# Reworked first and last stages, an earlier bias row, and the first MoE weight loaded ahead of the fifth and later x tiles, in a macaron transformer layer

## The reference

```python
x = x + 0.5 * ffn(layernorm(x))            # first MoE stage
x = x + attn(layernorm(x))                 # attention block with its own MLP
x = x + 0.5 * ffn(layernorm(x))            # second MoE stage, same weights

def ffn(x):                                # sq_relu(h) = relu(h)**2
    shared = sq_relu(x @ Ws1) @ Ws2        # 1024 -> 512 -> 1024
    top_vals, top_idx = top_k(x @ Wr, 2)   # 8 experts
    prob = trunc(softmax(top_vals))        # 1 only if a weight reaches 1.0
    return shared + (expert outputs weighted by prob)

def attn(t):
    q, k, v = t @ Wq + bq, t @ Wk + bk, t @ Wv + bv            # 16 heads of 64
    S = (q k^T - dist_scale * |i - j|) / sqrt(64), with a mask on (key, head) pairs
    h = layernorm(t + softmax(S) v @ Wo + bo, ln1)
    return layernorm(relu(h @ W1 + b1) @ W2 + b2 + h, ln2)     # 1024 -> 4096 -> 1024
```

## Time and profile before

| | us |
|---|---|
| median of 3 runs | 1446.87 |
| lowest and highest run | 1446.06, 1447.27 |
| the profiled execution | 1446.01 |
| its span, slowest core (core 6) | 1442.9 |
| its fastest core (core 7) | 1429.0 |
| PE, DVE, ACT busy on core 6 | 1279.6, 787.6, 833.9 |

### The profile page before, as it was taken

One profiled execution on the slowest core, in us unless ns is written; L12 is line 12 of the kernel. 1 busy time (PEld: TensorE's weight loads), 2 busy tenths in 40 slices (PEclk: granted clock), 3 DMA queues, 4 the chain that ended last, 5 costly groups with the idle time before them and its releaser, 6 DMA issues.

```text
span 1442.9 us, 20405 instructions; the slowest of 8 cores (1429.0 to 1442.9 us)
## 1 busy us (share of the span) xinstructions
PE 1279.6 (89%) x6458; PEld 616.9 (43%) x6580; DVE 787.6 (55%) x1272; ACT 833.9 (58%) x1173; POOL 38.3 (3%) x68
## 2 busy tenths in 40 slices
PE   3769879999989999999799999988999999789984
PEld 2334324444433644444346444444544444455442
DVE  5845314554457734459685443786834439680074
ACT  4555447777755766766557567665665666522311
POOL 1010200000000000000000000000000000000000
PEclk9979999999999999999999999999999999999997
DMA  9956999999923521314554222156431323685443
GB/s 229 210 109 133 167 127 128 133 118 128 137 61 106 157 96 64 120 62 147 182 154 146 67 87 92 55 179 201 135 121 62 110 77 85 191 248 176 149 140 109
DMA packets 115216, 187.66 MB, mean 130 GB/s; under 512 B 55822, under 2 KB 92692, under 8 KB 104088
## 3 DMA queue, kind: packets, MB, share of 16 engines
q1 hardware_dynamic: 86536, 154.74, 35.6%
q0 software_dynamic: 28560, 31.45, 17.9%
HBM read 178.86 MB, written 45.09 MB: 155 GB/s over the span
## 4 chain that ended last, share of the span: by engine, by line
PE 70%; DVE 9%; ACT 7%; issue 7%; DMA 3%; SPq 1%; another core or an unknown queue 1%; DVEq 0%; ACTq 0%
PE PS L243 70%; ACT EB L806 2%; DVE AT L846 1%; DMA HT<-SG 1%; DVE EB L812 1%; DVE sm L224 1%; DVE sm L226 1%; DMA VV<-x 1%; ACT RT L842 1%; ACT RT L840 1%; DMA Y<-SG 1%; ACT RT L843 1%; ACT H L1028 1%; SPq L66 1%
## 5 line engine op out<-in xcount | busy, mean ns | idle before, releaser
L806 ACT ACTIVATE EB<-PS 128x1024 bf16<-128x1024 f32 x512 | 520.6, 1021 | 312.7 <-PE PS L243 308.0
L812 DVE TENSOR_TENSOR EB<-EB,DP 128x1024 bf16<-128x1024 bf16 x512 | 352.0, 690 | 414.7 <-ACT EB L806 412.5
L243 PE MATMUL PS<-RG,H 128*128 128x512 bf16 x1251 | 306.7, 381 | 28.3 <-ACT H L1028 8.1
L243 PE MATMUL PS<-EB,VV 128*128 128x512 bf16 x988 | 298.5, 381 | 19.0 <-DVE AT L846 9.1
L243 PE MATMUL PS<-HT,RG 128*128 128x256 bf16 (+1 forms) x1647 | 283.3, 316 | 29.4 <-ACT H L1028 12.2
L243 PE MATMUL PS<-QP,KT 128*128 128x512 bf16 x1007 | 302.3, 380 | 5.4 <-ACT EB L806 3.0
L243 PEld LDWEIGHTS PS<-HT,RG 128*128 128x128 bf16 x1664 | 163.1, 99 | 137.8 <-issue 36.0
L243 PEld LDWEIGHTS PS<-RG,H 128*128 128x128 bf16 x1280 | 124.1, 98 | 186.3 <-issue 43.0
L243 PEld LDWEIGHTS PS<-QP,KT 128*128 128x128 bf16 x1024 | 99.9, 98 | 128.2 <-issue 10.0
L243 PEld LDWEIGHTS PS<-EB,VV 128*128 128x128 bf16 x1024 | 96.9, 98 | 126.7 <-issue 34.1
L1028 ACT ACTIVATE H<-PS,sm 128x256 bf16<-128x256 f32 (+1 forms) x176 | 98.3, 567 | 69.0 <-PE PS L243 68.7
(11 more groups left out here) (124 smaller groups left out, 825.7 us busy)
## 6 DMA issues: line engine op xcount, KB each, us to landing
RG<-wcW SPq DMA_DIRECT2D x64, 1024.0 KB, 5.4
RG<-wcWo SPq DMA_DIRECT2D x8, 1024.0 KB, 8.4
wcW<-W1a POOLq DMA_DIRECT2D x8, 1024.0 KB, 21.6
wcW<-W2a POOLq DMA_DIRECT2D x8, 1024.0 KB, 19.0
Y<-x1sp SPq DMA_DIRECT2D x16, 512.0 KB, 4.2
XT<-x1sp SPq DMA_DIRECT2D x16, 512.0 KB, 4.2
RG<-wcS SPq DMA_DIRECT2D x8, 1024.0 KB, 5.7
out<-Y SPq DMA_DIRECT2D x16, 512.0 KB, 3.3
```

The costliest lines, as they stand in the source:

```text
L243: return s.on("tensor", lambda e: e.matmul(out, lhsT, rhs, start=first, stop=last, skip_group_check=True), wait=wait, inc=inc)
L806: te = s.on("scalar", lambda e: e.activation(eb, po, AF.Exp, bias=-12.0, scale=1.0), wait=[tm, self.e_free[k], self.tok_consts])
L812: self.tok_p[k] = s.on("vector", lambda e: e.tensor_tensor(eb3, eb3, dp, ALU.mult), wait=[te, self.tok_dp])
```

## The change

1. Ws1 is loaded by two POOL DMAs of half its rows; x tiles 4 to 15 on SP wait for the first of them. Ws2 waits for x tile 7 (was 3), Wv for x tile 9 (was 7).
2. `wide` is loaded by eight SP DMAs of 496 columns behind the x tiles, no longer by POOL. `table` runs at k == 16 and also adds the two bias rows (`trw`), with the row's store and the load of GC behind it on SP; these stood after the loop.
3. The POOL load of the first half of Wq waits for the last transpose of stage A (tr2[15]), and the second half of Wk stands behind it.
4. In stage B the first K and Q projections are emitted first; a POOL no-op waits for the first K projection (all four parts) before Wq1 and the casts of `wc`.
5. `out_row` is emitted in `proj_stream` before head pair 6, not after pair 7, and the rest of the Q projections is reordered around it.
6. Squares of the last MoE are ACT instructions (AF.Square) in all blocks. For b = 3 the x1 rows are loaded into four places of KT, with the bias added ahead; `ln3_out` follows its own statistics at once; the MoE runs on tiles (0,1), (2), (3); of the router, the flag is computed from 16 columns, the four table operations follow the flag, and the last tile's two additions stand within the router.

The core of the diff:

```diff
@@ router
+        if mid is not None:
+            mid()
         v(lambda e: e.tensor_single_scalar(self.rden, self.rd, 1.0, ALU.add), [te])
...
-        v(lambda e: e.tensor_tensor(PR3, LT3, bc(self.v2), ALU.is_ge))
-        v(lambda e: e.tensor_tensor(PR3, PR3, bc(self.rw), ALU.mult))
-        v(lambda e: e.tensor_tensor(eq3, eq3, bc(self.rp1), ALU.mult))
-        v(lambda e: e.tensor_add(self.PR, self.PR, self.eq1))
+        v(lambda e: e.tensor_add(self.rden, self.rp1, self.rw))
...
+        t = v(lambda e: e.tensor_reduce(fm, self.rden, AX.X, ALU.max))
@@ phase_a
+                x_tok.append(s.dma("sync", "x%d" % i, xs[i], self.x0_d[128 * i:128 * i + 128, :], wait=wait))
...
+        tws = [s.dma("gpsimd", "ws1%d" % h, as8(sws1)[:, 4 * h:4 * h + 4, :], src1[:, 4 * h:4 * h + 4, :])
+               for h in range(2)]
...
-        load(4, 16)
+        load(4, 16, wait=[tws[0]])
...
-        twd = s.dma("gpsimd", "wide", wide, self.widea_d)
+        twds = []
+        for j in range(0, WIDE, 496):
+            twds.append(s.dma("sync", "wide%d" % (j // 496), wide[:, j:j + 496], self.widea_d[:, j:j + 496]))
...
-            if k == 14:
+            if k == 16:
                 table()
             if k - ROW2 - 1 == 11:
-                for j, w in ((2, self.Wk_d), (3, self.Wq_d)):
...
+                self.tok_ring[2] = s.dma("gpsimd", "r2", as8(self.slot(2)), piece(self.Wk_d, 0, 0),
+                                         wait=x_left[8] + x_left[9])
             if k - ROW2 - 1 == 15:
+                self.tok_ring[3] = s.dma("gpsimd", "r3", as8(self.slot(3)), piece(self.Wq_d, 0, 0),
+                                         wait=x_left[10] + x_left[11] + [tr2[15]])
@@ proj_stream
         for p in range(1, 8):
+            if p == 6:
+                yield from self.out_row(s)
@@ post_rows
+            XT = [self.KT[:, 2 * D * k:2 * D * k + 2 * D].bitcast(F32) for k in range(4)]
+            for tt in range(4):
+                t = self.x1_again(s, b, tt, XT[tt], [self.q_used[31]])
+                txs[tt] = s.on("vector", lambda e, x=XT[tt]: e.tensor_add(x, x, gc[:, D:2 * D]),
+                               wait=[t, self.tok_gc])
...
+            if not self.lagging:
+                self.ln3_out(s, b, HTt, *late)
+                late = None
@@ post_fill
-        for lo in (0, 2):
+        for lo, hi in ((0, 2), (2, 4)) if b < 3 else ((0, 2), (2, 3), (3, 4)):
...
-                th = s.on("vector", lambda e, hf=hf: e.tensor_mul(hf, hf, hf), wait=[t])
+                th = s.on("scalar", lambda e, hf=hf: e.activation(hf, hf, AF.Square), wait=[t])
...
+                tflag, table = self.router(
+                    s, [tlt], 1, lambda: [self.moe_out(s, b, tt, dh, *outs[dh]) for dh in range(2)])
...
+                table()
@@ phase_b
+        for tq in range(4):
+            for _ in self.proj(s, "k", 0, tq):
+                pass
+        for _ in self.proj(s, "q", 0, 0):
+            pass
+
+        s.on("gpsimd", lambda e: e.nop(), wait=[self.tok_k[0]], inc=False)
         self.ring_load(s, self.tok_v_pe)
```

More of the change, by code:

```diff
@@ L244, in mm, with router @@
                                                  skip_group_check=True), wait=wait, inc=inc)
-    def router(self, s, wait, k):
+    def router(self, s, wait, k, mid=None):
         LT3 = self.LT.rearrange("p (t e) -> p t e", e=8)
@@ L772, in proj_stream @@
             yield from self.proj(s, "q", p, 0)
-            if p < 7:
+            if p < 6:
                 for tq in range(1, 4):
                     yield from self.proj(s, "q", p - 1, tq)
-        yield from self.out_row(s)
+        for tq in range(1, 4):
+            yield from self.proj(s, "q", 5, tq)
         for tq, p in ((2, 6), (3, 6), (2, 7), (3, 7)):
@@ L1101, in post_fill @@
                 self.ht_free = [tm, tx]
-                if b == 3:
-                    tflag = self.router(s, [tlt], 1)
-            for tt in (lo, lo + 1):
-                i = 4 * b + tt
+            for tt in range(lo, hi):
+                outs = []
                 for dh in range(2):
```

114 lines of the change are left out of this document (63 added, 51 removed).

## The result

The changed kernel took 1425.99 us (median; 1425.78, 1425.99 and 1427.46), the kernel before, on the same chip, 1446.46. The ratio is 0.9862, with a 95% interval of 0.9842 to 0.9881: 20 us gained, 6 fewer than forecast.

A forecast was written before the change was run, and what follows sets the result against it. PE bounds attention; only stalls at four places could move. The slowest core, 3: 1439.7 - 10.3 - 2 - 2.2 - 1 - 10 = 1414.2, plus 2 for scatter, 3.1 outside and 0.9 to the median: 1420 us; range 1409 to 1434.

The forecast's parts named there:

- The table: Distance table in stage A: ACT's wait for the constant goes; -13 us in core 6, -6.6 core 1, -10.3 core 3.
- First matmul: Start of stage A: with Ws1 ahead of the fifth x tile, the first up matmul begins earlier; -2 us, 0 to -3.5.
- End of stage A: Last transposes, freed of casting loads, stop holding PE; -6 us in core 6, -7 core 1, -2.2 core 3.
- After the branch: Start of stage B: bulk casts come after K projection 0; -1 us, bounds -3 and +2.
- The seam: Between attention blocks 0 and 1: out_row's one-partition operations come two head pairs earlier; -4 us, -1 to -7.
- Squares: MoE of blocks 0 to 2: squares go from DVE to ACT; +0.5 us, bounds -1 and +3.
- Last stage: Last MoE and router: shorter chain, split pair, flag 8.1 us earlier; -6.5 us, bounds -3 and -9.
- The slowest core: Whole span: core 3 ends last at 1414.2 us, plus 2 for scatter of loads, making 1416.
- rivals, 1: Value tiles in stage A: the wait moves to Wv and the first transpose; 1429 us, up to 1434; chance 0.18.
- Rival 3: ACT squares: Square is not in the loaded table set, so each costs two table loads; 1485 us; chance 0.05.
- Rival 2: More gained: transposes never stop PE, branch 3 us shorter, seam gives 7; 1409 us; chance 0.14.
- Rival 4: Stalls only change places: later waits for loads or full queues give back the start's gain; 1446 us; chance 0.05.

The follow-up runs named there:

- e11: The changed kernel without x tiles 4 to 15 waiting for Ws1's first half, and with Ws1 as one transfer: 1424.5 us, ratio 0.9817.
- e6: The kernel before with only the changes to stage A and to what follows the branch; out_row, squares and last stage as before: 1430.1 us.
- e8: The changed kernel with the half of Wq loaded beside the half of Wk again, three iterations before the last transposes: 1429.7 us, ratio 0.9879.
- e9: The changed kernel with the bulk casts issued after the branch before K projection 0 again: 1426.6 us.
- e10: The changed kernel with the distance table's constant back on POOL's queue behind Wv and the table two iterations sooner: 1432.3 us, ratio 0.9863.

## Why the prediction was right in direction and 6 us too low

The range held, at 1426 between 1409 and 1434; the forecast of 1420 lay 6 below. That the sum came this near owes something to luck: several terms are right only added up. What went as said and what did not, by its own steps:

- **The table** (-13, core 1 -6.6, core 3 -10.3): right where I made the sum, at the value tiles: alone 10.5 on the mean, and with the other edits 13.2 (89.6 to 76.4). Wrong further on, since 4 of the 10.5 had been cover for DVE. I named no step in which the rest of stage A takes such a gain back.
- **First matmul** (-2): 0, by e11. The bound "later x tiles eat it" is what happened: up comes 1.0 sooner with the edit, the first value tile 0.6 later.
- **End of stage A** (-6): 9.4 at the flag, 4.2 at the first score. I costed Wq's later start at nothing, with 15 us of cover for its consumers. The consumers did have it. What had none is the stretch behind the branch, where PE stands some 3.5 longer with these loads in flight; I take it that the loading of instructions is what they hold up, which is argued (below).
- **After the branch** (-1): 0.
- Together the four were to give 22 in core 6, 16.6 in core 1 and 15.5 in core 3, and gave 24.7, 18.0 and 12.8. The sum was right and the shares were not, which is luck as much as insight: undone one at a time, the four make 6.2 - 0.9 + 4.2 + 0.2 = 9.7 of the 15.9 on the mean. Where the other 6 lie wasn't tried. It may be that each stall that is left covers part of the next, as the table's did; and the later starts of Ws2 and Wv and the earlier bias rows were in every one of these kernels.
- **The seam** (-4, -1 to -7): +1.0 in the changed kernel's trace, +5.3 in core 6. **This is one of the two steps that failed.** I counted out_row's DVE operations and not the DMA that it issues first, though its place on SP moved as well: from 21 us ahead of its use to 3 us ahead, behind q stores and beside casting loads. Without that wait the term is -1.7 on the mean, since the gap of 5.60 is also spread, not gone.
- **Squares** (+0.5, -1 to +3): +4.4 (3.4 to 5.2). **The other step that failed.** The duration was nearly right (0.38 taken, 0.42 measured); what was not is the likely case, "beside a PE that is fed by others", at 0.5. My worst case, a third of 9 us, was nearly the truth: 3.8 of 10.0, and 4.4 in the changed kernel. The way was another than the one I priced: PE's waits in the stretch add up to the same (48.6 after, 48.8 before), but some became longer, and 47 matmuls instead of 26 ran at half rate behind them. The term had no clock in it, though two others of mine had.
- **Last stage** (-6.5): -5.6 in the changed kernel, -7.5 alone. The size was right by luck. The recorded working doesn't give it: 1417.6 + 14.2 - 2 - 1.6 + 2 is 1430.2, not the 1428.5 that I wrote, so that my own parts make -4.8 and not -6.5. And the parts were off: I set 2 gained against 2 lost for the split pair, and it gives 4.7. The flag came 5.5 earlier on the mean (counted from the 32nd normalisation), not 8. The other parts (bias and squares off the chain, four operations out of the router) make up the 1 to 3 left.
- **The slowest core.** Core 3 set the end both in the forecast and in fact, at 1424.2 rather than 1414.2 and the 2 for scatter. It had less at the start than its term (-12.7 for -15.5), +3.6 between for my -3.5, and -6.4 in the tail: 1439.7 - 12.7 + 3.6 - 6.4 = 1424.2. What lies outside the span fell from 3.1 to 1.6.

Of the signs I had named, most came: ACT's wait of 2.04, the value tiles by 80, the last transposes in 3.0 with no gap of PE before the flag, two table loads. Two did not: the seam has a gap over 5 us, and the flag is less than 8 earlier. Of the rivals, 1 came near in time (1429) but not in cause: no value tile of any core waited for a transpose or a load. The turn-taking of queues that the Trainium skill, "DMA: Bandwidth & Descriptors", section "Queues, rings and completion order", states would make the Wv loads later with the constant in front; if it did, the two iterations of DVE work covered it, and no wait in the trace shows it. Rival 3 is out: two table loads stand in the whole execution, each of 1.28. The Trainium skill, "ScalarE: Activation LUTs", section "Table sets: the hidden batching unit", doesn't name square among the functions found in every set; in this kernel no load stands between the squares and the exps and logarithms around them. Rival 2 is out, since neither the branch nor the seam gained. Rival 4 is out by e6.

What stays open: whether the 4 us between flag and matmul are the instruction packets' own wait behind the casting loads, or the engines' wait for something else that the loads hold up. That the gap is short where no load is in flight (e8, and before up to its first matmul) and long where one is (the changed kernel, e9, e10 and e11) is shown, the link in between is argued. A kernel that has Wq landed before the branch without touching the last transposes was not tried.

## What to carry to other kernels

When a step is moved, look first at the DMA that it issues and waits for, where that now stands on its queue and how long before its use, and only then at its operations: here a row of 4 KB issued 178 us sooner was worth 2.1 us on the mean, more than the move itself (1.5). Price work moved to another engine by what that engine's queue holds up, not by its busy share. Compare PE's idle time and its busy time before you call a loss a wait: here the waits only became fewer and longer, and the time went into slower matmuls behind them. And where the last unit of a chain waits for a transfer, a smaller last piece lets the next to last fill the wait (4.7 here).

## What the runs showed of the hardware

- A row of 4 KB took 13.3 us from issue to use while casting loads held 98.1% of the DMA engines' time (core 6, 315 to 350 us); stores of q of 128 KB took 12.2 there. Small was not short here.
- The last two DMA transposes of stage A took 3.0 each with no casting load in flight and 14.9 and 12.1 beside one, in two kernels that differ only in where two loads are issued (core 6, changed kernel and e8).
- With casting loads in flight the first matmul behind the branch comes 8.7 after the flag on the mean, 5.2 without (e8), and the first score 21.5 and 16.4 after it.
- Behind each of the 16 waits of PE of 3.4 us (changed kernel, from the tenth to the 32nd normalisation, eight cores) matmuls of 512 columns start 0.43 apart instead of 0.22; four then take 1.91 instead of 1.03, with a granted clock of 0.57 (core 5, 689.8 to 693.8). Two stretches with the same idle time, 48.6 and 48.4, differ by 5.0 us in length.
- A Square of 128x256 bf16 takes 0.42 on ACT, against 0.38 for the relu from PSUM ahead of it and 0.29 for the product on DVE.
